# A new order for the prologue of a fused transformer block, its weights loaded in two parts, and groups of four added matmuls ahead of TensorE's steps

## The reference

```python
x = x + tanh(g_xattn) * xattn(layernorm(x), ctx, ctx, Wq, Wk, Wv, Wo, bo)
x = x + tanh(g_ffn)   * ffn(layernorm(x), w1, w2, h1, h2, w3, and their scales)

# xattn: 16 heads of 16, causal mask
qh, kh, vh = q @ Wq, k @ Wk, v @ Wv
scores = where(causal, qh @ kh.T / sqrt(16), -1e9)
out = softmax(scores) @ vh            # heads side by side
xattn = out @ Wo.T + bo
# ffn: the weights are -1, 0 or 1, with a scale for each output
h = silu(x @ w1.T * s1) * (x @ w2.T * s2)     # 256 -> 1024
h = gelu(h @ h1.T * t1)                       # 1024 -> 1024
h = gelu(h @ h2.T * t2)                       # 1024 -> 1024
ffn = h @ w3.T * s3                           # 1024 -> 256
```

## Time and profile before

| | us |
|---|---|
| median of 3 runs | 1783.74 |
| lowest and highest | 1782.88, 1784.28 |
| the profiled execution | 1783.53 |
| its span | 1781.2 |
| TensorE busy | 1721.5 |
| VectorE busy | 1319.0 |
| ScalarE busy | 1310.2 |
| GpSimd busy | 1098.3 |

### The profile page before, as it was taken

One profiled execution on the slowest core, in us unless ns is written; L12 is line 12 of the kernel. 1 busy time (PEld: TensorE's weight loads), 2 busy tenths in 40 slices (PEclk: granted clock), 3 DMA queues, 4 the chain that ended last, 5 costly groups with the idle time before them and its releaser, 6 DMA issues.

```text
span 1781.2 us, 39684 instructions
## 1 busy us (share of the span) xinstructions
PE 1721.5 (97%) x11078; PEld 1471.0 (83%) x11078; DVE 1319.0 (74%) x2803; ACT 1310.2 (74%) x3022; POOL 1098.3 (62%) x1647
## 2 busy tenths in 40 slices
PE   4599999999999999999999999999999999999998
PEld 3488888888888888888888888888888888888886
DVE  4877777777777777777777778777787777777763
ACT  3778777778777778777777777777777777777773
POOL 3567656667656667656657655656755656765652
PEclk7699999999999999999999999999999999999999
DMA  8644444444444544444544444444344454444420
GB/s 298 202 121 112 121 130 135 141 131 113 115 135 130 147 132 114 114 132 131 142 143 111 118 127 135 137 141 115 115 123 135 135 141 121 115 124 130 118 60 7
DMA packets 362523, 229.29 MB, mean 129 GB/s; under 512 B 274688, under 2 KB 332288, under 8 KB 360960
## 3 DMA queue, kind: packets, MB, share of 16 engines
q1 hardware_dynamic: 360336, 217.14, 43.4%
q10 hardware_dynamic: 2160, 11.81, 1.7%
HBM read 113.53 MB, written 41.94 MB: 87 GB/s over the span
## 4 chain that ended last, share of the span: by engine, by line
PE 92%; issue 2%; DMA 1%; DVE 1%; ACT 1%; POOL 1%; SPq 1%; POOLq 0%; ACTq 0%; DVEq 0%
PE ffn L984 71%; PE work L924 13%; PE s_bank L959 3%; PE pv L975 3%; PE work L1064 2%; SPq L357 0%; DMA q_saved<-q_parts 0%; DMA aw<-in_attn_w 0%; DMA xT<-in_x_T 0%; POOL hb L516 0%; ACT probs L824 0%; SPq L361 0%; DMA k_saved<-k_parts 0%; DVE full L654 0%; POOL ha L511 0%
## 5 line engine op out<-in xcount | busy, mean ns | idle before, releaser
L984 PE MATMUL ffn<-hb,W 128*128 128x512 f32 x2048 | 504.3, 399 | 1.3 <-POOL hb L516 1.3
L661 DVE TENSOR_REDUCE full<-ffn 128x256 f32<-128x512 f32 x512 | 349.5, 688 | 180.1 <-PE ffn L984 175.7
L984 PE MATMUL ffn<-ha,W 128*128 128x512 f32 x2048 | 479.9, 391 | 1.2 <-POOL ha L511 1.2
L984 PEld LDWEIGHTS ffn<-ha,W 128*128 128x128 f32 x2048 | 378.0, 188 | 80.9 <-POOL ha L511 2.4
L984 PEld LDWEIGHTS ffn<-hb,W 128*128 128x128 f32 x2048 | 375.2, 188 | 82.1 <-POOL hb L516 8.8
L824 ACT ACTIVATE probs<-probs,exp_bias 128x128 f32<-128x128 f32 x1024 | 320.3, 390 | 42.6 <-POOL exp_bias L479 41.5
L471 POOL TENSOR_TENSOR p_parts<-probs,p_parts 128x512 f16<-128x512 f32 x256 | 299.1, 1168 | 20.5
L984 PE MATMUL ffn<-x2T_hi,W 128*128 128x256 f32 x1024 | 260.2, 290 | 1.0 <-DVE x2T_lo L757 0.5
L516 POOL TENSOR_TENSOR hb<-full,hb 128x256 fp32r<-128x256 f32 x256 | 187.8, 739 | 112.4 <-ACT full L842 104.8
L984 PE MATMUL ffn<-x2T_lo,W 128*128 128x256 f32 x1024 | 254.3, 284 | 0.0
L842 ACT ACTIVATE full<-full,cols 128x256 f32<-128x256 f32 x512 | 253.2, 494 | 0.0
(11 more groups left out here) (86 smaller groups left out, 2432.5 us busy)
## 6 DMA issues: line engine op xcount, KB each, us to landing
k<-k_saved SPq DMA_DIRECT2D x256, 128.0 KB, 2.7
q<-q_saved SPq DMA_DIRECT2D x256, 128.0 KB, 2.7
k_saved<-k_parts SPq DMA_DIRECT2D x32, 512.0 KB, 2.9
q_saved<-q_parts SPq DMA_DIRECT2D x32, 512.0 KB, 2.9
wnat<-in_ffn_w ACTq DMA_DIRECT2D x11, 1024.0 KB, 6.4
xT<-in_x_T SPq DMA_DIRECT2D x32, 256.0 KB, 3.3
cT<-in_ctx_T SPq DMA_DIRECT2D x32, 256.0 KB, 3.4
x_in<-in_x SPq DMA_DIRECT2D x32, 256.0 KB, 3.6
```

The costliest lines, as they stand in the source:

```text
L661: dve.tensor_reduce(full[:, m % 4], src[:].rearrange("p (a t) -> p t a", a=2), AX_X, ALU.add).then_inc(done, 1)
L984: return pe.matmul(dst, w, h, **flags)
```

## The change

The diff, word for word in its parts with code:

- PROLOGUE has its steps in another order. Steps of two new kinds are in it: G.k, in which ScalarE issues the load of chunk k, and C.k, in which VectorE tests it. W.k is now ScalarE's rounding alone. The loads of chunks 0 and 1 are the first steps, behind the Tanh of the gates; none is issued ahead of it.
- aw comes in two DMAs, Wq and Wk first, Wv and Wo behind x_in, with a semaphore for each.
- TensorE does four matmuls of 128x128 float32 on two constant tiles, ident and mean_of, ahead of each step S, PV, To, O and X2 of the prologue. They write columns of the bank ffn0 that nothing reads; they wait for nothing. There are 10 + 8 + 2 + 2 + 2 = 24 such groups.

```diff
+IDLE_WORK = 4
...
 PROLOGUE = steps("""
-    Q.0 k q.0 q.1 W.0 st i.0 W.1 v K Q.1 e.0 i.1 V W.2 S.0 kw qw e.1 S.1 W.3 kr.0 i.2 S.2 S.3 Q.0+ s.0 m.0 p.0 qr.0
...
+    G.0 st G.1 rx q.0 q.1 k Q.0 i.0 W.0 qw v K C.0 i.1 W.1 C.1 s.0 p.0 m.0 Q.1 q.0+ V s.1 G.2 i.2 e.0 Q.0+ S.0 S.1
...
-        attn_w_in = sem("attn_w_in")
+        attn_w_in, value_w_in = sem("attn_w_in"), sem("value_w_in")
...
-            sp.dma_start(aw[:].rearrange("p w k e -> p (w k e)"), attn_w[:, :]).then_inc(attn_w_in, 16)
+            half = 2 * KE * E
+            sp.dma_start(aw[:, 0:2].rearrange("p w k e -> p (w k e)"), attn_w[:, 0:half]).then_inc(attn_w_in, 16)
             load_c(0)
             load_x(0)
+            sp.dma_start(aw[:, 2:4].rearrange("p w k e -> p (w k e)"), attn_w[:, half:2 * half]).then_inc(value_w_in, 16)
...
-                if kind == "W" and weights:
+                if kind == "C" and weights:
...
-            for i in range(STAGES):
-                load_chunk(i)
             act.wait_ge(gates_loaded, 16)
...
-                if i > 0 and i + STAGES - 1 < CHUNKS:
-                    load_chunk(i + STAGES - 1)
...
+                    if kind == "G" and weights:
+                        load_chunk(k)
...
+                    if isinstance(n, int) and n == 0:
+                        pe.wait_ge(value_w_in, 16)
...
+                        if weights and kind in ("S", "PV", "To", "O", "X2"):
+                            for _ in range(IDLE_WORK):
+                                pe.matmul(ffn[0][:, P:2 * P], ident[:], mean_of[:], start=True, stop=True)
```

More of the change, by code:

```diff
@@ L34 @@
 PROLOGUE = steps("""
-    Q.0 k q.0 q.1 W.0 st i.0 W.1 v K Q.1 e.0 i.1 V W.2 S.0 kw qw e.1 S.1 W.3 kr.0 i.2 S.2 S.3 Q.0+ s.0 m.0 p.0 qr.0
-    lr p.1 s.1 m.1 R.0 T.0 rx s.2 K+ m.2 W.4 s.3 p.2 q.0+ S.4 W.5 i.3 i.4 e.2 W.6 PV.0 R.1 T.1 s.4 m.3 S.5 qr.1 m.4
-    p.3 s.5 lc+ i.5 W.7 kr.1 m.5 s.6 i.6 Q.1+ p.4 PV.1 p.5 S.6 i.7 nm.0 m.6 nh.0 T.2 nm.1 S.7 T.3 lt+ p.6 s.7 PV.2
-    e.3 R.2 lx+ PV.3 T.4 k+ qw+ T.5 PV.4 qr.0+ p.7 PV.5 T.6 e.4 e.5 R.3 m.7 To.0 q.1+ nh.1 O.0 e.6 st+ R.4 W.8 R.5
-    nh.2 V+ W.9 W.10 to.0 PV.6 T.7 F.0 e.7 o.0 S.0+ PV.7 To.1 R.6 F.1 nh.3 kw+ R.7 nm.2 s.0+ kr.0+ n2.0 O.1 nm.3
-    X2.0 X2.1 v+ m.0+ to.1 i.0+ o.1 x2.0 kr.1+ n2.1 rx+ S.1+ lr+ x2.1 s.1+ e.0+ qr.1+ m.1+
+    G.0 st G.1 rx q.0 q.1 k Q.0 i.0 W.0 qw v K C.0 i.1 W.1 C.1 s.0 p.0 m.0 Q.1 q.0+ V s.1 G.2 i.2 e.0 Q.0+ S.0 S.1
+    m.1 S.2 p.1 S.3 s.2 K+ kw Q.1+ m.2 p.2 T.0 i.3 G.3 S.4 p.3 s.3 lr s.4 PV.0 e.1 lt+ q.1+ S.5 G.4 T.1 C.2 qr.0 e.2
+    kr.0 T.2 PV.1 lc+ R.0 k+ i.4 T.3 m.3 m.4 kr.1 W.2 C.3 qr.1 G.5 R.1 lx+ e.3 s.5 S.6 m.5 W.3 S.7 nh.0 PV.2 C.4 G.6
+    qw+ T.4 i.5 S.0+ S.1+ PV.3 s.6 T.5 R.2 C.5 qr.0+ PV.4 p.4 p.5 st+ e.4 C.6 W.4 kw+ T.6 s.7 m.6 G.7 i.6 i.7 PV.5
+    To.0 m.7 O.0 e.5 R.3 C.7 W.5 PV.6 W.6 R.4 G.8 V+ nh.1 T.7 p.6 nm.0 G.9 PV.7 e.6 W.7 G.10 To.1 nm.1 e.7 R.5 kr.0+
+    R.6 O.1 s.0+ C.8 m.0+ nh.2 C.9 W.8 p.7 o.0 C.10 i.0+ to.0 nh.3 nm.2 nm.3 R.7 v+ F.0 o.1 n2.0 to.1 W.9 kr.1+ F.1
+    lr+ n2.1 qr.1+ W.10 x2.0 x2.1 s.1+ rx+ X2.0 X2.1 m.1+ e.0+
 """)
```

## The result

| | before | changed |
|---|---|---|
| median, us | 1783.37 of 9 runs | 1792.00 of 9 runs |
| lowest and highest | 1780.58, 1784.46 | 1787.04, 1795.69 |
| the profiled execution | 1783.53 | 1795.11 |
| its span | 1781.2 | 1792.8 |
| first feed-forward matmul of block 1 | 82.61 | 95.50 |

The ratio is 1.0046, 95% interval 1.0032 to 1.0060: the change costs 8.6 us. The forecast was 1782.0, between 1778.2 and 1786.3; the result lies outside, above, and the likeliest sign was wrong too. The changed kernel's runs are also spread over 8.6 us, those of the kernel before over 3.9. One execution of each kernel in that measurement (4888 us before, 5585 us changed) stands far apart from all others and is left out of its medians and ratios.

What follows compares the result with a forecast made beforehand. The prediction took TensorE as the bound from block 1 on, so only the prologue's end and the clock there could move: 1783.5 + 0.7 (later first feed-forward matmul) - 2.2 (clock) = 1782.0 us, range 1778.2 to 1786.3.

Steps and rivals of the forecast that it cites:

- the likeliest sign: Whole kernel: the forecast of 1782.0 us lay below the kernel before's profiled 1783.53 us.
- The tail: Flag to block 1's first feed-forward matmul: 3.7 us warm or 5.9 at clock 0.50; next block's scores there cost nothing before.
- the prediction's own sum: Prologue's end: mask at 28.5, 43.8 us of work, 6.2 of waits, then the tail; first feed-forward matmul at 83.3.
- VectorE's work: From the first scores' mask to the last x2T_lo: 45.0 us of work, plus waits summing to 6.2 us.
- waits of over 9 us: Sign that the forecast is wrong: VectorE's waits between 28 and 79 us sum to under 4 or over 9.
- The first scores: Prologue's S.0 at 28.0, 3.4 us earlier (between 0 and 5), with chunk 2 issued only at about 24.
- The first weights: Prologue's start: first half of aw waited for until about 6.3 us, 1.25 us less, ends 0 and 2.5.
- The added matmuls: 24 prologue groups at 1.7 us (1.2 GHz) or 0.85 us (2.4 GHz) each, costing nothing where the step waits longer anyway.
- The clock: Block 1's start: clock at 1.0 at once or 2 us later instead of 5.8; 2.2 of 2.5 us gained.
- Groups on the path: Rival, prologue: groups at clock 0.50 delay ready steps by 1.7 us each; 1785.9, up to 1788; chance 0.26.
- 0.72 for the same: Whole kernel: chance that the time lies between 1780.2 and 1787.3 us, within about 0.2% of no change.
- 0.08 for slower: Whole kernel: chance that the time lies over 1787.3 us.

Runs made afterwards that it cites:

- the second: The second profiled execution of the unaltered changed kernel, from measuring it once more against other runs of the kernel before; that measurement's ratio is 1.0030.
- e14: Changed kernel with chunk loads 3 to 10 cut to 512 of 2048 columns, so the result's values differ; ratio 1.0009.
- e12: Changed kernel with VectorE's chunk tests 1 to 10 over 512 of 2048 columns, 17 us less work; ratio 1.0049.
- e5b: Changed kernel with the next block's scores and their masks late again, and chunk 2's load right behind chunk 1's; ratio 1.0018.
- e2b: Kernel before, its order and loads kept, with 21 of the 24 groups of added matmuls; ratio 1.0011.
- e7: Kernel before with eight added matmuls ahead of each of X2.0 and X2.1 only; ratio 0.9998.
- e8: Changed kernel up to T.4, then the kernel before's sequence, with two weight loads and 21 groups; ratio 1.0047.
- e11: Kernel before with the attention weights in two loads and eight added matmuls ahead of X2.1 only; ratio 0.9990.
- e4: Changed kernel with chunk 2's load issued right behind those of chunks 0 and 1; ratio 1.0045.
- e1: Changed kernel without its 24 groups of added matmuls, order and split load kept; ratio 1.0045.
- e3: Changed kernel with scores S.0+ moved behind PV.5 and S.1+ behind X2.1, the mask s.0+ left early; ratio 1.0048.
- e6: Kernel before with only the load of the attention weights split in two halves; ratio 0.9992.

## Why the prediction was wrong

**The step that failed** is the remark in "The tail" that the next block's scores, now ahead of it, cost nothing before. It asked what they cost, and not when their inputs come. They were moved ahead of PV.3 on an engine on which nothing overtakes, while their k is written, read back and placed through the DMA queues in the middle of the chunk loads. The wait at S.0+ was in no term and in no rival. In the first execution it is 8.2 us, and with the two scores and their groups at 1.2 GHz (66.90 to 71.30) PV.3 is 13.0 us late; in the second 8.1. e14 shows that the chunk loads are what makes the transfers long, and e12 that VectorE's tests don't make the wait. e5b, with these scores and masks late, is at 1.0018 against 1.0046 and 1.0030: between two and three fifths of the loss goes with them.

In the prediction's own sum, for the first execution: the first mask at 32.6 us instead of 28.5 (+4.1), VectorE's work 43.0 instead of 43.8 (-0.8), its waits 12.0 instead of 6.2 (+5.8), and from there to the first feed-forward matmul 7.9 instead of the 4.8 midway between 3.7 and 5.9 (+3.1). That is 95.5 instead of 83.3; with 0.9 us less gained by the clock it gives the 1795.1 measured.

**VectorE's work** was counted as what the end waits for: 45.0 us of work and 6.2 of waits. The work was right (43.0 us from the first mask to inexact, 43.8 forecast); the waits up to there are 12.0 us in the first execution, of which 3.5 for S.4 (3.1 forecast) and 5.2 for nh.1 behind S.0+ (2.5 with C.8). But e12 shows that in this kernel the sum was of the wrong engine: without 17 us of it the end doesn't move (low_all at 86.5 instead of 85.3). It is the right engine only for e5b. The prediction had named waits of over 9 us as a sign that it is wrong, and so they were.

**The tail** was forecast as 3.7 to 5.9 us from the flag to the first feed-forward matmul; from inexact, 87.57, it took 7.9. VectorE reads the flag only behind the residual, the moments and x2n (1.5 us), for which TensorE waits 2.0 us ahead of the group, and the clock has fallen to 0.50 by then, at 89.1. With groups in place the tail is 5.0 to 6.1 us where the flag is read well ahead of X2.0 (e2b, e7, e8, e11), and 7.6 to 9.7 where it is summed behind O.1. At a clock of 1.00 throughout, it is 5.0 to 6.1 (e7, e8, e11) against 7.6 (e4, e12), so that the position of the flag costs about 2 us by the table and a clock that falls there up to 2 more. No edit moved the flag forward by itself. In the first execution other distances behind PV.3 are shorter by as much (14.5 us to O.1 instead of 18.9), so that it didn't add to the 13.

**The first scores** were forecast at 28.0. Six more executions with the same table up to there have S.0 between 27.6 and 30.3, most at 28; the first has 31.75. "Chunk 2 is issued only at about 24", so that it doesn't collide, was wrong: it was issued at 23.62, the k placements between 22.0 and 24.5. The executions say what that costs: where chunk 2 is issued 1.3 or 1.6 us behind the first k placement (the two of the changed kernel), S.0 comes 8.8 and 9.7 us behind that placement; where it is 2.2 us or more (e1, e3, e8, e12, e14), 5.3 to 6.6. But e4 shows that the gain is not carried through anyway: whatever is early there waits at S.0+.

**The first weights** were right: 6.30 us (6.3 forecast). e6 puts the effect on the whole time at 1.4 us, with an interval that takes in no difference; of the 1.25 us forecast 0.4 arrives at its first feed-forward matmul.

**The added matmuls** were priced right, 0.95 us a group at 2.4 GHz and 1.71 at 1.2 (0.85 and 1.7), and neutral in the changed kernel (e1) as far as the intervals tell. In "The clock" a gain of 2.2 us was taken; the rest of the program was 1.3 us shorter in the first execution, where block 1 still began with 3.7 us at 0.50, and 3.5 us in the second. In e6, with no group, it was 1.7 us shorter as well, so that not all of such a gain is the groups'.

In the earlier trace rows TensorE has waits of 2 to 4 us spread over the prologue. The Trainium skill, TensorE: Matmul & The Clock Gate, section "Why this matters for your kernels", asks that gaps between bursts be avoided; e7 and e11 agree, with block 1 at 1.00 from its first matmul. The rest is shorter by 1.1 to 3.5 us in the profiles with groups, and the whole is still 5 to 8 us slower.

**The rivals.** "Groups on the path" had the right side, and a price of 1785.9 up to 1788, but its mechanism was not the main one: e1, without the groups, loses as much. Something of it is there, since the groups cost 1.8 us in e2b and 2.4 us behind S.0+ in e1's comparison. The wait at S.0+ was missing. The chances of 0.72 for the same and 0.08 for slower were made from the spread of a sum that left out a wait of 8 us.

**What stays open:** why the medians of e1 and e3 lie 4 to 6 us above their own profiled executions. The changed kernel's two profiles differ in when the k placements land, and e1 and e3 have the same loads, but no second profile of theirs was taken. For the same reason it is open where in the prologue e5b gains what its ratio shows. e5b moves the scores, their masks and chunk 2's load together, and e3 and e4 are no sum of it. How much the order of VectorE's tests alone costs in the changed kernel can't be read from e8.
